# Where a gated decoder block prepares the weights of its second cross attention

## The reference

```python
def _L1_xattn_ref(hidden_states, encoder_hidden_states, Wq, Wk, Wv, Wo, bo):
    ...                                   # 16 heads of 64
    q = hidden_states @ Wq
    k = encoder_hidden_states @ Wk
    v = encoder_hidden_states @ Wv
    ...
    scores = jnp.einsum('bhsd,bhkd->bhsk', q, k) * scale
    probs = jax.nn.softmax(scores, axis=-1)
    out = jnp.einsum('bhsk,bhkd->bhsd', probs, v)
    out = out.transpose(0, 2, 1, 3).reshape(B, S, H * Dh)
    out = out @ Wo + bo
    return out
...
x = x + jnp.tanh(g_ffn[0]) * _L0_ffn_ref(_layernorm(x, axis=-1), ...)
x = x + jnp.tanh(g_xattn[1]) * _L1_xattn_ref(_layernorm(x, axis=-1), ctx_768, ...)
```

## Time and profile before

| | us |
|---|---|
| median of 3 runs | 2001.97 |
| lowest and highest run | 2001.23, 2002.74 |
| profiled execution: its own time | 2003.22 |
| profiled execution: span from first to last instruction | 2001.4 |
| setup block | 0 to 36.6 |
| block of the sum | 899 to 934 |
| second cross attention: its block opens | 934.0 |

### The profile page before, as it was taken

One profiled execution on the slowest core, in us unless ns is written; L12 is line 12 of the kernel. 1 busy time (PEld: TensorE's weight loads), 2 busy tenths in 40 slices (PEclk: granted clock), 3 DMA queues, 4 the chain that ended last, 5 costly groups with the idle time before them and its releaser, 6 DMA issues. The chain is left out here.

```text
span 2001.4 us, 37718 instructions
## 1 busy us (share of the span) xinstructions
PE 1762.3 (88%) x11570; PEld 1339.4 (67%) x11570; DVE 1517.2 (76%) x3061; ACT 1146.6 (57%) x2941; POOL 1166.7 (58%) x1158
## 2 busy tenths in 40 slices
PE   3688877799999999994899999996789997799998
PEld 2355555588888888872677777775535555588886
DVE  5699978677887787767666766675769997677876
ACT  1366645555555555552677777775436666455554
POOL 4777736567776777655233333323768884667764
PEclk9699977799999999995999999998869997799999
DMA  5111100555556566430000000000000000222222
GB/s 126 47 45 46 48 17 14 129 137 136 146 143 144 129 145 146 128 83 8 5 5 5 5 5 5 1 1 1 0 1 1 0 1 17 72 79 64 82 66 69
DMA packets 99645, 115.22 MB, mean 58 GB/s; under 512 B 18064, under 2 KB 55120, under 8 KB 99504
## 3 DMA queue, kind: packets, MB, share of 16 engines
q1 hardware_dynamic: 96576, 112.14, 21.7%
q10 hardware_dynamic: 2928, 1.39, 0.3%
HBM read 101.82 MB, written 3.28 MB: 53 GB/s over the span
## 5 line engine op out<-in xcount | busy, mean ns | idle before, releaser
L76 POOL TENSOR_TENSOR b_moe_hid_low<-b_moe_hid,b_moe_hid_high 128x512 fp32r<-128x512 f32 x256 | 331.3, 1294 | 173.2 <-ACT b_moe_hid_high L1038 171.5
L1044 ACT ACTIVATE bank<-bank 128x512 f32<-128x512 f32 x384 | 223.5, 582 | 339.8 <-PE bank L83 339.8
L1744 POOL TENSOR_TENSOR XC<-XC,c_recip 128x480 f32<-128x480 f32 x128 | 126.8, 991 | 292.6 <-DVE c_recip L1911 292.6
L1069 DVE TENSOR_TENSOR b_moe_gu<-bank,XC 128x512 f32<-128x512 f32 x256 | 176.6, 690 | 115.7 <-PE bank L83 100.0
L76 POOL TENSOR_TENSOR e_moe_hid_low<-e_moe_hid,e_moe_hid_high 128x512 fp32r<-128x512 f32 x128 | 165.6, 1294 | 84.2 <-ACT e_moe_hid_high L1038 83.4
L1865 ACT ACTIVATE XC<-bank,c_shift 128x120 f32<-128x120 f32 x512 | 176.9, 364 | 21.2 <-DVE c_shift L1901 21.2
L71 DVE CAST c_ts_high<-bank 128x480 fp32r<-128x480 f32 x128 | 84.2, 658 | 135.0 <-PE bank L83 134.3
L1074 DVE TENSOR_TENSOR b_moe_hid<-bank,b_moe_gu 128x512 f32<-128x512 f32 x256 | 176.9, 691 | 9.3 <-POOL b_moe_hid_low L76 0.7
L1038 ACT ACTIVATE b_moe_hid_high<-b_moe_hid 128x512 fp32r<-128x512 f32 x256 | 160.0, 625 | 12.4 <-DVE b_moe_hid L1074 11.6
L1860 ACT ACTIVATE c_probT<-bank 120x512 f32<-120x512 f32 x128 | 76.6, 598 | 105.1 <-PE bank L1790 103.2
L1069 DVE TENSOR_TENSOR e_moe_gu<-bank,XC 128x512 f32<-128x512 f32 x128 | 88.4, 690 | 62.2 <-PE bank L83 51.0
(11 more groups left out here) (386 smaller groups left out, 5622.9 us busy)
## 6 DMA issues: line engine op xcount, KB each, us to landing
XC<-b_comb SPq DMA_DIRECT2D x256, 256.0 KB, 4.4
XC<-e_comb SPq DMA_DIRECT2D x64, 256.0 KB, 3.1
X<-in_x SPq DMA_DIRECT2D x4, 512.0 KB, 9.0
a_att_qs_high<-XC SPq DMA_DIRECT2D x32, 64.0 KB, 1.8
a_att_qs_low<-a_Q_low SPq DMA_DIRECT2D x32, 64.0 KB, 1.9
a_att_ks_high<-a_K_high SPq DMA_DIRECT2D x32, 64.0 KB, 1.9
a_att_ks_low<-a_K_low SPq DMA_DIRECT2D x32, 64.0 KB, 1.9
b_moe_w_gate<-in_b_wgT SPq DMA_DIRECT2D x8, 256.0 KB, 3.0
```

Source lines behind the costliest of these rows:

```text
L76: return eng.tensor_tensor(low.bitcast(F32R), x, high, ALU.subtract)
L1044: act.activation(gate_b[j % 4][:], gate_b[j % 4][:], ACT.Silu).then_inc(s_silu, 1)
L1069: dve.tensor_tensor(gu[j % 2][:], up_b[j % 2][:], comb[j // 2][:, (j % 2) // share, :], ALU.mult).then_inc(s_gu, 1)
L1744: pool.tensor_tensor(prob[r % 8], prob[r % 8], recip[:, r % 8, :].unsqueeze(2).broadcast_to([P, HG, NKV]), ALU.mult).then_inc(s_norm, 1)
```

## The change

The loads of `wkT` and `wqT`, the 16 head products and their copies leave the setup block. The block of the sum gets a SyncE list with three loads (first context, `wkT`, `wqT`); TensorE makes one group of head products in each of the steps t = 1 to 4, into banks 4 to 7; ScalarE writes each group twice from there, as `mT` and as its high part, and makes the high parts of `c_wv`, of the first context and of `c_wo`; GpSimd makes the low parts. The attention block starts without this work. The bias is no longer added in the block of the sum but on GpSimd inside the attention, in the 13th of each 16 slots, and VectorE waits for it before it adds a quad's result. Some tiles of the attention (`vs`, `probT`, `ysum`) now lie in `YT`, whose content is used up by then.

```diff
@@ setup block
-                load(sp, wkT[:], w["c_wkT"].rearrange("(h p) e -> p h e", p=C_DH), s_load)
-                load(sp, wqT[:], w["c_wqT"].rearrange("(h p) d -> p h d", p=C_DH), s_load)
...
-                for g in range(NG):
-                    act.wait_ge(s_mt, g + 1)
-                    act.activation(mT[:, HG * g:HG * g + HG, :], bank[g][0:DC, :].rearrange("p (h d) -> p h d", h=HG),
-                                   ACT.Copy, scale=C_DH ** -0.5)
...
@@ block of the sum
+            @block.sync
+            def _(sp):
+                sp.dma_start(raw[:], ctxT[0:4].rearrange("b e t -> e b t")).then_inc(s_ctx, 16)
+                sp.dma_start(wkT[:], w["c_wkT"].rearrange("(h p) e -> p h e", p=C_DH)).then_inc(s_wkq, 16)
+                sp.dma_start(wqT[:], w["c_wqT"].rearrange("(h p) d -> p h d", p=C_DH)).then_inc(s_wkq, 16)
+
             @block.scalar
             def _(act):
+                def weights(t):
+                    if t == 0:
+                        act.activation(wvp[0][:].bitcast(F32R), small["c_wv"][:], ACT.Copy).then_inc(s_wh, 1)
+                    if t == 1:
+                        act.wait_ge(s_ctx, 16)
+                        act.activation(csp[0][0][:].bitcast(F32R), raw[:], ACT.Copy).then_inc(s_ch, 1)
+                    g = t - 2
+                    if 0 <= g < NG:
+                        act.wait_ge(s_m, g + 1)
+                        products = m_b[g][0:DC, :].rearrange("p (h d) -> p h d", h=HG)
+                        act.activation(mT[:, group(g)], products, ACT.Copy, scale=C_DH ** -0.5)
+                        act.activation(mTs[0][:, group(g)].bitcast(F32R), products, ACT.Copy, scale=C_DH ** -0.5).then_inc(s_mh, 1)
+                    if t == 6:
+                        act.activation(wos[0][:].bitcast(F32R), c_wo[:], ACT.Copy).then_inc(s_oh, 1)
...
@@ its list for TensorE, behind the transposes of the sum
+                    g = t - 1
+                    if 0 <= g < NG:
+                        pe.wait_ge(s_wkq, 32)
+                        for j in range(HG):
+                            i = pe.matmul(m_b[g][0:DC, j * D:(j + 1) * D], wkT[:, HG * g + j, :], wqT[:, HG * g + j, :],
+                                          start=True, stop=True)
+                        i.then_inc(s_m, 1)
@@ its list for GpSimd, behind the root of step t
-                    q = t - 3
-                    if q >= 0:
-                        pool.wait_ge(s_scaled, q + 1)
-                        pool.tensor_tensor(X[:, 4 * q:4 * q + 4, :], X[:, 4 * q:4 * q + 4, :],
-                                           bo1[:].unsqueeze(1).broadcast_to([P, 4, D]), ALU.add)
+                    if t == 1:
+                        pool.wait_ge(s_wh, 1)
+                        keep_low(pool, wvp[1][:], small["c_wv"][:], wvp[0][:])
+                    if t == 2:
+                        pool.wait_ge(s_ch, 1)
+                        keep_low(pool, csp[0][1][:], raw[:], csp[0][0][:])
+                    g = t - 3
+                    if 0 <= g < NG:
+                        pool.wait_ge(s_mh, g + 1)
+                        keep_low(pool, mTs[1][:, group(g)], mT[:, group(g)], mTs[0][:, group(g)])
+                    if t == 7:
+                        pool.wait_ge(s_oh, 1)
+                        keep_low(pool, wos[1][:], c_wo[:], wos[0][:])
@@ attention block, GpSimd
-                low_keys(0)
-                low_context(0)
-                pool.wait_ge(s_wh, 1)
-                keep_low(pool, wvp[1][:], small["c_wv"][:], wvp[0][:]).then_inc(s_wl, 1)
-                for g in range(1, NG):
-                    low_keys(g)
-                pool.wait_ge(s_oh, 1)
-                keep_low(pool, wos[1][:], c_wo[:], wos[0][:]).then_inc(s_ol, 1)
...
+                    if n % 16 == 12 and 0 <= n // 16 < NQ:
+                        qd = n // 16
+                        pool.tensor_tensor(X[:, 4 * qd:4 * qd + 4, :], X[:, 4 * qd:4 * qd + 4, :],
+                                           bo1[:].unsqueeze(1).broadcast_to([P, 4, D]), ALU.add).then_inc(s_bias, 1)
@@ attention block, VectorE
-                high_context(0)
-                keep_high(dve, wvp[0][:], small["c_wv"][:]).then_inc(s_wh, 1)
...
                         dve.wait_ge(s_yturn, qd + 1)
+                        dve.wait_ge(s_bias, qd + 1)
```

More of the change, by code:

```diff
@@ L144, in build @@
         ident16 = sb("ident16", [P, P], BF16)
-        prep = ExitStack()
-        wkT = sb("wkT", [C_DH, H, DC], ctx=prep)
-        wqT = sb("wqT", [C_DH, H, D], ctx=prep)
-        s_mt = sem("m_ready")
         loads = []
@@ L187, in scalar @@
                 act.activation(tg[:], gates[:], ACT.Tanh).then_inc(s_tg, 1)
-                for g in range(NG):
-                    act.wait_ge(s_mt, g + 1)
-                    act.activation(mT[:, HG * g:HG * g + HG, :], bank[g][0:DC, :].rearrange("p (h d) -> p h d", h=HG),
-                                   ACT.Copy, scale=C_DH ** -0.5)
-            @staticmethod
-            def tensor(pe):
-                pe.wait_ge(s_load, all_loads)
-                for g in range(NG):
-                    for j in range(HG):
-                        h = HG * g + j
-                        last = pe.matmul(bank[g][0:DC, j * D:(j + 1) * D], wkT[:, h, :], wqT[:, h, :],
-                                         start=True, stop=True)
-                    last.then_inc(s_mt, 1)
             @staticmethod
@@ L247, in stats @@
                     block.scalar(setup.scalar)
-                    block.tensor(setup.tensor)
                 halves = [slice(0, NB // 2), slice(NB // 2, NB)]
@@ L733, in build @@
         stats("a_stat", bias=bo0, setup=Setup)
-        prep.close()
         assert len(loads) == many_loads
@@ L1541, in build, with parts, group @@
         experts("b_moe", XT, b_combD, s_stored, weights, E0 * I0 // P, 1, False, YT)
+        moe.close()
         renew_semaphores()
-        own = ExitStack()
+        cross = ExitStack()
+        def parts(name, shape, count=None):
+            if count is None:
+                return [sb(f"{name}_{part}", shape, ctx=cross) for part in ("high", "low")]
+            return [parts(f"{name}{i}", shape) for i in range(count)]
+        mTs = parts("c_mT", [DC, H, D])
+        wvp = parts("c_wvp", [DC, H * C_DH])
+        wos = parts("c_wos", [P, 8, D])
+        raw = sb("c_ctx", [DC, 4, NKV], ctx=cross)
+        csp = parts("c_csp", [DC, 4, NKV], 2)
+        def group(g):
+            return slice(HG * g, HG * g + HG)
+        own = ExitStack()
+        wkT = sb("cn_wkT", [C_DH, H, DC], ctx=own)
+        wqT = sb("cn_wqT", [C_DH, H, D], ctx=own)
+        mT = sb("cn_mT", [DC, H, D], ctx=own)
+        m_b = bank[4:8]
+        s_wkq = sem("cn_key_query_weights")
+        s_ctx = sem("cn_ctx_loaded")
+        s_m = sem("cn_key_products")
+        s_mh = sem("cn_key_weights_high")
+        s_ch = sem("cn_ctx_high")
+        s_wh = sem("cn_value_weights_high")
+        s_oh = sem("cn_out_weights_high")
         ys = [sb(f"cn_ys{i}", [P, 512], ctx=own) for i in range(2)]
@@ L1572, in _ @@
                         act.activation(ys[t % 2][:], YT[:, t * 512:t * 512 + 512], ACT.Copy, scale=tg[:, 2:3]).then_inc(s_ys, 1)
+                    weights(t)
                     q = t - 5
@@ L1598, in _ @@
                 pool.wait_ge(s_root, 1)
-                for t in range(NQ + 3):
+                for t in range(NQ):
                     if t < NQ:
@@ L1710, in build @@
         FIRST, LAST = -4, SLOTS + 14
-        def group(g):
-            return slice(HG * g, HG * g + HG)
         with nc.Block() as block:
@@ L1717, in _ @@
             def _(sp):
-                for qd in range(NQ):
-                    wait(sp, s_cl, qd)
+                for qd in range(1, NQ):
+                    wait(sp, s_cl, qd - 1)
                     sp.dma_start(raw[:], ctxT[4 * qd:4 * qd + 4].rearrange("b e t -> e b t")).then_inc(s_cs, 16)
@@ L1723, in _ @@
             def _(pool):
[L1724 to L1726 removed]
                 def low_context(qd):
[L1729 removed]
+                    pool.wait_ge(s_ch, qd)
                     keep_low(pool, csp[qd % 2][1][:], raw[:], csp[qd % 2][0][:]).then_inc(s_cl, 1)
[L1732 to L1739 removed]
                 for n in range(FIRST, LAST):
@@ L1757, in keys @@
                     if h == 0:
-                        pe.wait_ge(s_cl, m // NG + 1)
-                        if m < NG:
-                            pe.wait_ge(s_ml, m + 1)
+                        wait(pe, s_cl, m // NG)
                     wait(pe, s_kcopy, n + 4)
@@ L1841, in _ @@
             def _(act):
-                def high_keys(g):
-                    act.activation(mTs[0][:, group(g)].bitcast(F32R), mT[:, group(g)], ACT.Copy).then_inc(s_mh, 1)
-                for g in range(NG):
-                    high_keys(g)
-                act.activation(wos[0][:].bitcast(F32R), c_wo[:], ACT.Copy).then_inc(s_oh, 1)
                 for n in range(FIRST, LAST):
@@ L1925, in _ @@
```

(2 more changed lines are left out.)

49 lines of the change are left out of this document (12 added, 37 removed).

## The result

| | before | changed |
|---|---|---|
| median of 12 runs, us | 2001.43 | 2006.94 |
| lowest and highest run | 1997.37, 2004.42 | 2003.86, 2011.30 |
| first profiled execution: own time | 2003.22 | 2004.19 |
| its span | 2001.4 | 2002.4 |

The ratio is 1.0028, with a 95% interval of 1.0019 to 1.0037: the changed kernel is slower by 5.5 us (3.8 to 7.4). The forecast was +2.5 us. The measured median lies in the range that was given, but beyond the 4.0 us up to which I had called it the same; the interval begins just inside them.

The account below looks back on a forecast made before the run. TensorE was taken as 88% busy on average, with VectorE's chain setting the end of the block of the sum. Setup -1.06, attention's opening -4.73 and block +8.25 gave +2.5 us: 2004.4 us, range 1999.5 to 2008.5.

Parts of the forecast that it names:

- Setup, 1.06: Setup block: without loads, products and copies it ends with GpSimd's last cast at 35.31, not 36.37; 1.06 us gained.
- The attention's opening, 4.7: Attention block: the 4.83 us before TensorE's first key product go, 0.1 us allowed to start; 4.7 us gained.
- the end contention, 0.4: End of the block of the sum: GpSimd's low part of c_wo hits only the seventh quad's scaling; 0.4 us gained.
- Landing of the weights, 7.4 us behind the opening: Block of the sum: both weight loads in at 906.4, at 190 GB/s behind the context, with TensorE waiting.
- A group of products, 1.7 us: TensorE in the block of the sum: each group of four head products takes 1.7 us, between transposes.
- The hold under the low part of wvp, 0.7 us: Block of the sum: GpSimd's low part holds VectorE's scaling of the first quad from about 916.8 to 917.5.
- The bias in the attention, 0: Attention: eight bias additions of 1.27 us on idle GpSimd cost 0; with no cover 10 us.
- the term for the block: Block of the sum: sixth addition 8.65 us later, less 0.4 us gained at the end; 8.25 us later.
- The first (longer stall): Rival: TensorE waits longer for the weights in the block of the sum, up to 2009.3 us; chance 0.17.
- The second: Rival: weights in at 904.9 and 2.4 GHz behind the stall in the block of the sum; -1.0 us, chance 0.15.
- The third (all hidden, -6.2): Rival: block of the sum hides all added work, weights there by 902; -6.2 us, 1995.8 us, chance 0.06.
- The bounds of the arrival: Block of the sum: weights in between 904.9 and 911.3 instead of 906.4, moving the total by -1.5 to +4.9 us.

Follow-up runs that it names:

- e1: Changed kernel with head products made from long-loaded tiles, so TensorE doesn't wait for the weight loads; ratio to the kernel before 1.0004.
- e5: Changed kernel with the two weight loads back in the setup block, products left in the block of the sum; ratio to the kernel before 1.0003.
- e6: Changed kernel with its added work laid into the engines' idle gaps, some low parts in the attention's opening; 1995.70 us, ratio to the kernel before 0.9968.
- e2: Changed kernel with the head products, their copies and low parts three steps later (t = 4 to 7); ratio to the kernel before 1.0009.

## Why the prediction was right or wrong, point by point

- **Setup, 1.06.** Measured 1.03 in the first pair of traces; over all traces with and without the product there, 21.1 to 21.9 against 20.1 to 20.4. Right, and a little small.
- **The attention's opening, 4.7, and the end contention, 0.4.** Behind the sixth addition 29.08 - 23.79 = 5.29 us were saved, against 5.1. Right; the low part of `c_wo` held the seventh scaling, which took 2.74 us.
- **Landing of the weights, 7.4 us behind the opening.** 8.31: 0.9 late, and the largest single miss; 7.79 and 8.44 in the two repeats, so 0.4 to 1.0 late. With the opening at 897.9, where the prediction put it, they are in at 906.2, inside the 904 to 907 outside of which I had called myself wrong. From the context's landing at 898.7 to that of `wqT` at 904.2 the 917 thousand bytes moved at 166 GB/s in the mean. My 190 is a rate while loads are moving, and left out the tail, in which the last packets land and little else moves. The Trainium skill's page "DMA: Bandwidth & Descriptors", section "Anatomy of one DMA — SWDGE (gpsimd) path", gave an estimate of 4.5 us for the same bytes by its fit for another issuing path; the measurement is 7.8 to 8.4 and decides, for these loads of short runs from SyncE's queue.
- **A group of products, 1.7 us.** 1.95 (904.31 to 906.26). I had taken it from the setup block, where the groups stand back to back and their weight loads take 6.79 us for four, 1.70 each. Here they take 1.67 us, and another 0.28 pass before the first weight load of the transposes. It is that switch, and not the clock, that I left out (last section). That is 0.25 us on the third addition (+7.25, not +6.1) and 0.2 on each step (2.99, not 2.8).
- **The hold under the low part of wvp, 0.7 us.** About 0.44, which is the variance's 0.61 us in place of the 0.17 it takes undisturbed; the scaling then started at 915.72 and took its 1.10. So the low part held the variance in front of the scaling, and not the scaling itself. With all this the sixth addition is 10.0 us late, not 8.65.
- **The bias in the attention, 0.** Right: nobody waits for it, and the attention is no longer than the old one.
- **The sum.** -1.03 + 4.71 = +3.7 us from these two stretches in the first pair of traces, where I had +2.5; with three traces of each kernel -1.31 + 4.69 = +3.4. The spans of that first pair differ by only 1.0 us, because the untouched loops happened to be 2.5 us shorter in the changed one: the two spans alone would have hidden most of it. The mechanism, one wait of TensorE for the weights with the additions queued behind it, was the right one, and e1 and e5 price it at 4.9 us. What was mis-sized is the term for the block: 8.25 us less the 4.73 of the opening is +3.5, and it measured +4.7. Two of its sizes did it, landing (0.9) and group (0.25, and 0.2 on each of two steps); the hold gave 0.2 back.
- **The median, +5.5.** Some 2 us of it are in no step. The interval begins at 3.8 us, just above the traces' sum. The scatter of the untouched parts is as large, and no trace pins the difference to a place: this stays open. The median lies in my range because that was made wide for the rivals; no step of mine foresaw these 2 us.
- **Rivals.** The first (longer stall) named the right direction, but its point of 9.0 us behind the issue was not reached (8.44 at most). The second put 2.0 us on a rise of the clock behind the stall; it stayed at 0.50. It also had groups and transposes halve at the high clock. Transposes do nearly so (1.12 us for four at 0.50, 0.63 at 1.00, 905.86 in the kernel before); no run has a group of head products at a clock that is shown to be 1.00 (last section), so for the groups it stays open. The third (all hidden, -6.2) is the size that e6 reached (-6.3), but by another order, and not by an early landing.
- **The chances.** A forecast of +2.5 us left 1.5 us to the bound of 0.2%. An error of 0.9 us in one landing and of 0.25 in a group takes most of that, so 0.72 for "same" was too much. The interval, 3.8 to 7.4 us, reaches just below the bound; that it does is luck and not to the credit of the sum. The bounds of the arrival, -1.5 to +4.9 us, were in the text; they stood in the range and hardly in the chances.

## What to carry to other kernels

A transfer that is issued where a block opens should have its first reader no earlier than its bytes at the rate of such runs, with start and tail: here 7.8 to 8.4 us for 1.1 MB; and on an in-order queue the wait holds all that stands behind it, also work that needs nothing of the transfer. Work that is to hide in a block has to be laid into the gaps of each engine, out of the way of the engine that sets the end: nearly the same instructions cost 44.5 us in one order and 32.6 in another, with three of the low parts moved behind the first key product. A profile against a profile can differ from the medians by some us; comparing stretches between fixed events shows which part of it belongs to the change.

## What the runs showed of the hardware that I had not expected

- **The hold between GpSimd and VectorE.** A low part on GpSimd (two inputs, 512 columns or more) stretched a scaling to 2.74 or 4.92 us from 1.10, and even a 128x4 variance to 0.61 from 0.17. The roots on GpSimd (128x4, 1.03 us) beside a scaling left it at 1.11. The Trainium skill's page "SBUF — State Buffer", section "SBUF: two separate sides", says that GpSimd and VectorE share a pair of ports by an exclusive lock. The scaling at 932.66 agrees with that: it ended at 935.40, 0.85 us or three of its four operations behind the end of the low part at 934.55. That of e2 ended at 934.53, 0.59 us or two of its four behind the third low part at 933.94. That the roots don't hold it is not what I would read out of the page.
- **The clock in one program is not the same from execution to execution.** In the kernel before it rose 20, 20 and 36 us behind the first key product, and the attention took 453.1, 453.2 and 457.1 us. The loops, with no instruction changed, took 823.7 to 829.8 us over the fourteen traces.
- **The rows give a clock of 1.00 to work that ran at the speed of 0.50.** In the setup block and until 40 us every stage of the kernel before reads 1.00. Yet the eight transposes at 38.40 loaded their weights in 226 ns and multiplied in 417 (medians), as the transposes at 899.8 do with the clock at 0.50 (230 and 421); with a recorded rise to 1.00, at 905.8, they take 143 and 273. So the setup's 1.00 doesn't tell what that work ran at. The head products there take the same as in the block of the sum at 0.50 (280 against 276 ns a weight load, 418 against 414 a matmul), which fits 0.50 in both places. The weight loads of the kernel before (smallest, median and largest time in ns), in the order of this text:

```profile
L336 PEld LDWEIGHTS bank<-ident,a_xn x8: 183/226/229, 38.4 to 39.7; 128*128 128x128 f32 x8
...
L1585 PEld LDWEIGHTS bank<-ident,cn_ys x10: 180/230/230, 899.8 to 901.8; 128*128 128x128 f32 x10
...
L1585 PEld LDWEIGHTS bank<-ident,cn_ys x4: 141/143/143, 905.8 to 906.1; 128*128 128x128 f32 x4
...
L199 PEld LDWEIGHTS bank<-wqT,wkT x32: 229/280/280, 28.6 to 35.1; 64*96 64x96 f32 x32
```

those of the head products in the changed kernel:

```profile
L1620 PEld LDWEIGHTS bank<-cn_wqT,cn_wkT x32: 230/276/282, 904.3 to 914.7; 64*96 64x96 f32 x32
```

and the stage of the eight transposes at 38.40, with its 1.00 (columns as in the earlier trace rows):

```profile
38.40:40.00 1.60, 1.60 (x8) 1.60 (x9) 0.54 (x1) 0.45 (x1) 0.00 (x0) 1.00 0.51 138
```
